# A graph layer in one program: folded mixer weights, centred key weights, split edge weights, and hot columns on ScalarE

## The reference

```python
xn = _layernorm(x, axis=-1)
x = x + gnn(xn, src, dst, edge_weight, ...) + mix(xn[None], ...)[0]
x = x + ffn(_layernorm(x, axis=-1)[None], ...)[0]

# gnn: new_x[src] += edge_weight * xn[dst]; then two 256x256 products around a batch norm and tanh
# mix: qkv = xn @ w_qkv + b_qkv; per head (8 heads of 32):
k = _ln(k, kln_g, kln_b); v = _ln(v, vln_g, vln_b)
kv = einsum('bhnd,bhne->bhde', k, v) / HW
out = einsum('bhnd,bhde->bhne', q, kv)
ret = out + xn
h = gelu(ret @ w1 + b1); mixed = h @ w2 + b2 + xn
# ffn: router over 8 experts, top 2, each expert 256 -> 1024 -> 256 with gelu
```

## Time and profile before

| | |
|---|---|
| median of 3 runs | 2387.26 us |
| the profiled execution | 2384.72 us |
| its span, from first to last instruction | 2383.3 us |
| first put, last put starts | 108.38 us, 1352.15 us |
| experts, full windows from | 1700 us |
| mean granted TensorE clock | 0.891 |

### The profile page before, as it was taken

One profiled execution on the slowest core, in us unless ns is written; L12 is line 12 of the kernel. 1 busy time (PEld: TensorE's weight loads), 2 busy tenths in 40 slices (PEclk: granted clock), 3 DMA queues, 4 the chain that ended last, 5 costly groups with the idle time before them and its releaser, 6 DMA issues. The chain is left out here.

```text
span 2383.3 us, 38273 instructions
## 1 busy us (share of the span) xinstructions
PE 1934.3 (81%) x11227; PEld 1607.3 (67%) x11251; DVE 1713.1 (72%) x5437; ACT 1128.4 (47%) x2236; POOL 1278.8 (54%) x811
## 2 busy tenths in 40 slices
PE   2559997697888878887877266985899999999995
PEld 1437775565665656656666134872799999999995
DVE  4848898687767858673333076888788888988884
ACT  1324443222232332323222114236899999999993
POOL 1447787578778877766777600000355444455542
PEclk8579998799998989888999598665899999999997
DMA  7878877477787787868888673223588888878885
GB/s 232 283 189 153 168 115 126 76 127 121 122 156 132 125 163 134 177 98 192 176 171 165 97 223 112 68 89 107 150 232 233 234 232 233 232 233 234 233 233 167
DMA packets 325710, 401.93 MB, mean 169 GB/s; under 512 B 34841, under 2 KB 267054, under 8 KB 325364
## 3 DMA queue, kind: packets, MB, share of 16 engines
q1 hardware_dynamic: 193822, 256.71, 34.9%
q0 software_dynamic: 103008, 103.83, 32.2%
q10 hardware_dynamic: 28662, 38.84, 5.3%
HBM read 251.12 MB, written 154.55 MB: 170 GB/s over the span
## 5 line engine op out<-in xcount | busy, mean ns | idle before, releaser
L1094 POOL DMA_INDIRECT acc_dram<-third x566 | 914.6, 1616 | 343.0 <-issue 138.6
L2016 POOL DMA_INDIRECT sum_dram<-node,small x112 | 198.2, 1770 | 316.4 <-DVE node L1945 222.7
L1873 PE MATMUL bank<-up_parts 128*128 128x256 f32 x2688 | 334.4, 284 | 2.3 <-DVE up_parts L1903 2.3
L1886 PE MATMUL bank<-down_parts 128*128 128x256 f32 x2688 | 335.4, 284 | 0.0
L1873 PEld LDWEIGHTS bank<-up_parts 128*128 128x128 f32 x2688 | 329.2, 193 | 2.7 <-DVE up_parts L1903 2.7
L1886 PEld LDWEIGHTS bank<-down_parts 128*128 128x128 f32 x2688 | 325.3, 191 | 0.0
L551 PE MATMUL bank<-work,third 128*128 128x256 f32 x1132 | 294.4, 403 | 27.8 <-ACT third L1049 27.7
L1049 ACT ACTIVATE third<-bank 128x512 f32<-128x512 f32 x283 | 168.6, 597 | 290.1 <-DMA acc_dram<-third 234.5
L857 DVE TENSOR_SCALAR third<-fixed,third 128x128 f32<-128x128 f32 x566 | 164.2, 369 | 161.0 <-PE bank L540 142.0
L1998 POOL DMA_INDIRECT node<-xh_dram,small x112 | 135.5, 1209 | 242.2 <-DVE small L1699 208.4
L551 PEld LDWEIGHTS bank<-work,third 128*128 128x128 f32 x1132 | 217.9, 205 | 63.9 <-ACT third L1049 31.6
(11 more groups left out here) (268 smaller groups left out, 3237.4 us busy)
## 6 DMA issues: line engine op xcount, KB each, us to landing
turned<-in_w_up SPq DMA_DIRECT2D x56, 1024.0 KB
turned<-in_w_down SPq DMA_DIRECT2D x56, 1024.0 KB
work<-src_dram SPq DMA_DIRECT2D x141, 256.0 KB
acc_dram<-fixed SPq DMA_DIRECT2D x15, 1280.0 KB, 13.2
work<-xn_dram SPq DMA_DIRECT2D x146, 128.0 KB
work<-acc_dram SPq DMA_DIRECT2D x72, 256.0 KB, 3.5
at_dram<-turned ACTq DMA_DIRECT2D x48, 256.0 KB
work<-at_dram ACTq DMA_DIRECT2D x24, 512.0 KB, 4.5
```

Source lines behind the costliest of these rows:

```text
L1094: e.indirect_dma_start(acc_dram[i], bass.IndirectOffsetOnAxis(put_i[:, t:t + 1], 0), M[:, t % (2 * QUAD), :], None, compute_op=ALU.add).th ...
L1873: k = e.matmul(ps, W1s[:, 2 * b + wp, q, h * P:(h + 1) * P], xTs[:, 2 * b + xp, q, :], start=(q == 0 and (wp, xp) == TERMS[0]), stop=(q == ...
L1886: k = e.matmul(bank[5 + c][:, 0:D], hTs[:, hp, h, c * P:(c + 1) * P], W2s[:, 2 * b + wp, h, :], start=(h == 0 and hp == 0 and wp == 0), st ...
L2016: e.indirect_dma_start(sum_dram, bass.IndirectOffsetOnAxis(slot_i[:, n:n + 1], 0), yb[:, i % 2, c, :], None, compute_op=ALU.add).then_inc( ...
```

## The change

It leaves the node stretch and the experts alone. In the first stretch:

- **Folded mix weights.** After the keys, two more steps multiply KV with the q weights and with Wm1, and add the product to Wm1 and to its bias; q, KV and `ret` are then gone from each chunk. Per chunk remain two up steps and two down steps; the up of chunk c+1 stands ahead of the down of chunk c, and banks and `hT_mix` are doubled.
- **Centred key weights.** The weights and the bias of k and v are centred once per head, so the sums and the centring of each key step go. ScalarE squares straight from the bank, and `kvn` has five slots, with a column of ones at each end.
- **fp32r halves.** The edge weight is split in a rounded part and a rest, in two fp32r matrices `one_lo`, made by one VectorE instruction; TensorE makes two fp32r products for a hot tile in place of one fp32 product.
- **ScalarE ones.** `one_hi` is made on ScalarE as Relu(1 - Abs(n - column)). A is cleared by ScalarE in 13 pieces, three steps long before the first group and piece by piece behind the copies later.
- The first group is 6 nodes wide (294 columns), not 5 (245). The row numbers take one table less, OH has three quads, and the costs by hand are new. M keeps two quads and `at_in` two slots.

The diff, cut to its core:

```diff
-DENSE = ((0, 108, 5), (108, 152, 6), (152, 188, 6), (188, 216, 7))
+DENSE = ((0, 108, 6), (108, 152, 6), (152, 188, 6), (188, 216, 7))
 S_QUADS = 3
+ROW_QUADS = 2
...
+    AI = 2
...
-        mix_steps = sum(3 * KC + (chunk(c)[2] // P) // 2 for c in range(NCH))
-        dense_cost = [2.0, 0.5, 0.5]
+        mix_steps = KC * NCH + sum(len(pair_of(c, m)) > 0 for c in range(NCH) for m in range(KC))
+        dense_cost = [0.6, 0.6, 0.6]
         for a, b, _ in DENSE:
-            dense_cost += [0.8] * (b - a + 2) + [0.7] * (-(-HI // 4) + 1)
+            dense_cost += [0.25] * (b - a + 3) + [0.2] * (-(-HI // 4) + 1)
...
-                in_turn, cost_in_turn, m = in_turn + [0], cost_in_turn + [1.65], m + 1
+                in_turn, cost_in_turn, m = in_turn + [0], cost_in_turn + [0.15], m + 1
...
-        costs = [2.0] + [2.8] * (NT + 4) + [1.0] * 2 + cost_in_turn + [2.4] * (2 * PRODUCTS)
+        costs = [0.6] * 3 + [0.9] * NT + [0.4] * 4 + [0.5] * 4 + cost_in_turn + [0.53] * (2 * PRODUCTS)
...
-                        e.matmul(dense_bank(n)[:, 0:HI * s], one_lo[:, t % 4, :], one_hi[:, t % 3, 0:HI * s],
-                                 start=True, stop=True).then_inc(s_ap, 1)
+                        e.wait_ge(s_away, HOT_DONE[t])
+                        for i_ in range(2):
+                            k = e.matmul(dense_bank(n)[:, 0:even(HI * s)], one_lo[:, t % 4, i_, :], one_hi[:, t % 3, 0:even(HI * s)],
+                                         start=(i_ == 0), stop=(i_ == 1))
+                        k.then_inc(s_ap, 1)
...
-                    e.tensor_reduce(ksum, rows, AX.X, ALU.add).then_inc(s_kvln, 1)
-                    e.wait_ge(s_kvln, KEY_DONE["sum", t])
-                    if t >= 4:
-                        e.wait_ge(s_kvacc, t - 3)
-                    e.scalar_tensor_tensor(out=d3, in0=spread16(ksum), scalar=-1.0 / HD, in1=rows,
-                                           op0=ALU.mult, op1=ALU.add).then_inc(s_kvln, 1)
...
+            for g in range(2):
+                e.wait_ge(s_foldp, g + 1)
+                e.tensor_copy(folded[:, g, :], bank[6 + g][:, 0:D]).then_inc(s_fold, 1)
+                e.tensor_copy(kvar2[:, 0, g:g + 1], bank[6 + g][:, D:D + 1]).then_inc(s_fold, 1)
+            yield
+            e.wait_ge(s_foldp, 3)
+            for m in range(KC):
+                e.tensor_tensor(Wm1[:, m, :], Wm1[:, m, :], bank[6 + m][:, 0:D], ALU.add).then_inc(s_fold, 1)
+            e.tensor_tensor(cols[:, 1, :], cols[:, 1, :], bank[5][:, 0:KC], ALU.add).then_inc(s_fold, 1)
+            yield
...
-            e.memset(A, 0.0).then_inc(s_tables, 1)
+            e.tensor_scalar(far_col, near, -1.0, 1.0, ALU.mult, ALU.add).then_inc(s_tables, 1)
...
-                        e.tensor_scalar(one_lo[:, t % 4, :], iota_p, lo_col[:, t:t + 1], w_c[:, t:t + 1], ALU.is_equal, ALU.mult)
-                        e.tensor_scalar(one_hi[:, t % 3, 0:HI * s], iota_n[:, 0:HI * s], hi_col[:, t:t + 1], None,
-                                        ALU.is_equal).then_inc(s_one, 1)
+                        e.scalar_tensor_tensor(out=one_lo[:, t % 4], in0=iota_p.unsqueeze(1).broadcast_to((P, 2, P)),
+                                               scalar=lo_col[:, t:t + 1], in1=parts_w[:, t, :].unsqueeze(2).broadcast_to((P, 2, P)),
+                                               op0=ALU.is_equal, op1=ALU.mult).then_inc(s_one, 1)
...
-                if g + 1 < NG:
-                    e.wait_ge(s_atp, HC4 * (g + 1))
-                    e.memset(A, 0.0).then_inc(s_clear, 1)
...
+                        e.activation(away[:, t % 2, 0:even(HI * s)], iota_n[:, 0:even(HI * s)], ACT.Abs, bias=far_col[:, t:t + 1]).then_inc(s_away, 1)
...
+                        e.activation(one_hi[:, t % 3, 0:even(HI * s)], away[:, t % 2, 0:even(HI * s)], ACT.Relu, bias=ones[:, 0:1],
+                                     scale=-1.0).then_inc(s_away, 1)
```

More of the change, by code:

```diff
@@ L163, in gps_layer @@
         third = region("third", NT * D, late)
-        work = region("work", 13064, late)
+        work = region("work", 13060 + NG, late)
         src_c = third(EG * P)
         w_c = third(EG * P)
-        trash_minus = third(EG * P)
         dup = third(EG * P)
@@ L360, in dense_bank @@
             return bank[n % 2]
[L363 to L367, removed]
-            mix_uses += [(s_mfin, 4 * c + j + 1) for j in range(chunk(c)[2] // P)]
-        USES = 3 * KC + 4
-        def mix_bank(n):
-            return bank[5 + n % 3]
         quat = [[(0, 1), (1, 1), (2, 1), (3, 1)], [(1, -1), (0, 1), (3, 1), (2, -1)],
@@ new lines, in keys_tensor, with up, down @@
+            for m in range(KC):
+                for g in range(2):
+                    k = e.matmul(bank[6 + m][:, 0:D], folded[:, g, m * P:(m + 1) * P], Wm1[:, g, :], start=(g == 0), stop=(g == 1))
+            k.then_inc(s_foldp, 1)
+            yield
+        def mix_tensor(e):
+            def up(c, m):
+                w = chunk(c)[2]
+                e.wait_ge(s_xr[c % 2], 16 * (c // 2 + 1))
+                if KC * c + m:
+                    e.wait_ge(s_mha, KC * c + m)
+                for q in range(KC):
+                    k = e.matmul(bank[5][:, 0:w], Wm1[:, q, m * P:(m + 1) * P], xnT_ring[:, c % 2, q, 0:w],
+                                 start=(q == 0), stop=(q == KC - 1))
+                k.then_inc(s_mh, 1)
+            def down(t):
+                c, j = t // 4, t % 4
+                e.wait_ge(s_mha, KC * (c + 1))
+                if t >= 2:
+                    e.wait_ge(s_mfin, t - 1)
+                for q in range(KC):
+                    e.matmul(bank[6 + t % 2][:, 0:D], hT_mix[:, c % 2 * KC + q, j * P:(j + 1) * P], Wm2[:, q, :],
+                             start=(q == 0), stop=False)
+                e.matmul(bank[6 + t % 2][:, 0:D], ones_b, b2_b, start=False, stop=True).then_inc(s_mfp, 1)
+            e.wait_ge(s_fold, 7)
+            for m in range(KC):
+                up(0, m)
+                yield
@@ L464, in mix_tensor @@
+                    if len(pair_of(c, m)):
+                        for t in pair_of(c, m):
+                            down(t)
                         yield
@@ L473, in dense_tensor @@
             for g, (a, b, s) in enumerate(DENSE):
-                for i in range(b - a + 2):
-                    t = a + i - 1
+                for i in range(b - a + 3):
+                    t = a + i - 2
                     if a <= t < b:
@@ L587, in keys_vector @@
                 vec.wait()
+                if row is b2row:
+                    for end in (0, 2 * D + 1):
+                        vec.done(e.memset(kvn[:, :, end:end + 1], 1.0))
+                    vec.wait()
                 e.scalar_tensor_tensor(out=row_b, in0=r, scalar=ident[:, 2:3], in1=row_b, op0=ALU.mult, op1=ALU.add).then_inc(s_bias, 1)
@@ L955, in mix_scalar, with clear @@
+                    if len(pair_of(c, m)):
                         yield
         def dense_scalar(e):
-            yield
-            yield
-            yield
-            for g, (a, b, s) in enumerate(DENSE):
-                for i in range(b - a + 2):
+            def clear(k):
+                block = A[:, 4 * k:min(4 * k + 4, HI), :].rearrange("p a b -> p (a b)")
+                return e.activation(block, zeros[:, 0:block.shape[1]], ACT.Copy)
+            e.wait_ge(s_set, SET_ZEROS)
+            e.wait_ge(s_xnTd, 16 * NCH)
```

382 lines of the change are left out of this document (192 added, 190 removed).

## The result

The change makes the kernel slower: 2440.64 us, the median of 4 runs (2438.05 to 2457.46), against 2386.06 us (2382.23 to 2388.74) in the same comparison; ratio 1.0245, interval 1.0197 to 1.0293. The profiled execution took 2439.76 us, its span is 2438.4 us, and its mean clock 0.858. The forecast of 2372 us was wrong, in sign too, and the range ended at 2425.

A forecast was written before the change was run, and what follows sets the result against it. GpSimd's puts, with a floor of 1.86 us each, were taken to bound the first stretch. Terms -11.5, -12, -6 and +17 sum to -12.5 us on 2384.7: 2372 us; 8 in 10 range 2325 to 2425.

The forecast's parts named there:

- The same chain: Hot quads: addition, `select` and `indices`, hot tile, product, base block and next product sum to 7.5 us, under GpSimd's 8.3.
- It has room; 0: ScalarE in hot quads: with Abs and Relu added it does 5.4 us per quad of 8.3; term 0.
- Keys now spread over 43 quads: Key steps: keys fall on 43 quads in place of 32, hidden by puts and landings; term 0, bounds 0 and -24.
- the count: Hot stretch: 216 tiles now fall on 51 quads, where before it was 2.7 on 80 quads.
- The share at half clock: Hot quads: 16% of 51 quads at the lower clock, 8 x 2.1 us: +17 us, bounds 0 and +107.
- rival A: Quads 46 to 96: the dense loop at half clock bounds the stretch, 2419 to 2462 us; chance 0.30.
- Clearing A on ScalarE: Hot stretch: two long puts beside VectorE's clearings go; -11.5 us, bounds 0 and -16.5.
- The rule on shared interfaces: Puts: GpSimd contends with VectorE's two-port or two-input instructions; for `one_lo` at most +91 us, left inside rival A's range.
- The transition: From 391 to 484 us: half of the 24 us lost there comes back, -12 us; bounds -6.7 and -24.
- the fold steps: In key quads: eight small instructions, once; 0.
- Centred keys: Key steps, 174 to 391 us: some 1.4 us of VectorE less per step, hidden; term 0, bounds 0 and -24.
- `ret` and KV gone: From 1020 to 1080 us: q, KV and `ret` go, up runs one chunk ahead; -6 us, bounds 0 and -12.

The follow-up runs named there:

- ring4: The changed kernel with ScalarE's Abs and Relu one tile further ahead, `one_hi` ring four deep, AT left at three slots: 2421.03 us, 1.0104 to the kernel before.
- select_between: The changed kernel with VectorE's program order alone changed, `select` and `indices` behind the tiles dealt ahead of the base block: 2369.57 us, 0.9894 to the kernel before.
- keys_first: The changed kernel with only the costs changed, key steps at half cost, products at 0.42: 2356.24 us, 0.9866 to the kernel before.
- before_hot_late: The kernel before with only its costs changed, key steps 1.7 times as costly, hot tiles dealt as the change deals them: 2477.7 us, 1.0399.
- hot_twice: The changed kernel with the two fp32r products of each hot tile issued twice: 2451.83 us, 1.0248 to the kernel before.
- clear_vector: keys_first with A cleared by VectorE again, four instructions in place of ScalarE's 13 pieces: 2373.1 us, 0.9936 to the kernel before.
- ones_vector: The changed kernel with `one_hi` made on VectorE again, nothing on ScalarE for it: 2436.61 us, 1.0183 to the kernel before.
- ones_ahead: The changed kernel with ScalarE's Abs and Relu two tiles further ahead, `one_hi` ring 5 not 3, AT 2 slots not 3: 2437.31 us, 1.0177 to the kernel before.

## Why the prediction was wrong, by its own steps

*"The same chain is ... 7.5 us. GpSimd needs 8.3 us per quad, so at full clock the loop keeps ahead."* This step failed. The 24 quads with two and two took 9.0 us at full clock and 10.9 at half, the 11 with three and two 10.7 at full clock. The chain as summed held VectorE and TensorE alone. In the quad from 847.24 to 857.60 us its term for the base block, "the next product and its start" and the addition is 2.62 + 0.5 + 0.46 = 3.6 us, and takes 5.5 there, with the wait for ScalarE's ones in it; `select` and `indices` take 2.9 for 2.74, `one_lo` and the second addition 1.3 for 0.88, and the product ahead of the block 0.7 for 0.3. "It has room; 0" for ScalarE went by its busy share: 5.4 us of 8.3. But its 1.08 us per tile stand between the copies into M and the next product, on the path. ring4 puts a price on that order: 20 us on the medians, 34 by the ratios (1.0245 against 1.0104). That `select` and `indices` stand ahead of the second addition was in the chain; what it costs was not seen, and select_between puts it at 71 us, with what the clock gives back.

*"Keys now spread over 43 quads ... Term 0"* failed with it. It was 0 on the belief that the puts set the pace everywhere. Where the hot tiles set it, their stretch takes its 580 us whatever the quads (586, 576, 583 and 591 us in the kernel before, the change, keys_first and before_hot_late), and each quad dealt elsewhere is added: 57 us for eight. The prediction had the two and two in front of it, and the 8.75 us between such blocks in the kernel before, but then went by the 7.5 us of its own sum. One gap was also too few to read: the five quads of this kind before took 9.9 us on the mean. And the count was off: the 216 tiles were said to move from 80 quads to 51, where by the programs 66 quads issue hot products before and 57 after.

*The share at half clock*, 16% of the quads, was read off a mean clock. Of the changed kernel's 53 quads with steps of hot tiles and no transposes 24 ran their block at half, and 0.84 in the windows is below the 0.86 that rival A named. Rival A, at a chance of 0.30, gave 2419 to 2462 us, and 2440 lies amid it; blocks over 10 us apart and puts that wait for the copies into M were its signs, and both came, but the clock was 0.84 and not near 0.6. Its cause holds in part: 17 of 24 quads with two and two were at half, but the 11 with three and two were slow at full clock, hot_twice raised the clock for nothing, and select_between took the wait away and found the clock risen by itself, to 0.89 from 530 to 1000 us. How much of the 71 us that it gave back is the clock and how much the wait is not parted. The Trainium skill, page "TensorE: Matmul & The Clock Gate", section "HAM oscillation — how this bites in real kernels", has such restarts in every pass of a loop with a wait. The trace agrees in part: 24 of these 53 blocks ran so, 1.91 us for 1.05, and the others at full clock.

*Clearing A on ScalarE*, -11.5, was right in mechanism: the changed kernel has no put over 2.1 us. The size is within what the runs can tell: 17 us by clear_vector, with three long puts; the kernel before has the two that were counted, at 722.55 and 869.64 us. The rule on shared interfaces ("GPSIMD Engine Reference", section "1. Specifications", of the Trainium skill) would fit the clearing if this memset runs in a two-port mode, which no run here shows. For the two-input `one_lo` no price shows: a put's mean is 1595 ns with it, and 1616 before, or 1596 without the 11.5 us of the two long puts.

*The transition*, -12, was half moved on. From 391 to 484 us 49 puts go where 33 went, but from 484 to 530 us 17 puts take 46 us, 12 more than at 2.0 each. There stand the fold steps, priced at 0 "in key quads", and the tables; no run parts them. GpSimd waits 5.98 us ahead of the put at 494.95:

```profile
494.95 1.56 POOL L1145 DMA_INDIRECT acc_dram<-third  x1 [5.98 <-DVE third L903]
```

*Centred keys*: 2.01 us per put for 2.09, some 9 us over 108 puts where the prediction had 0, within its bounds. *`ret` and KV gone*, -6: not seen apart from the rest; 1000 to 1177 us was slowed by the hot tiles.

## What to carry to other kernels

When a loop over several engines is dealt out from a table, the path inside one round decides, not any engine's busy share: write the round down once with every engine's program order, and look for what stands between a result and its user. A table of costs is an edit as large as any: here it was worth 87 us one way (before_hot_late) and 84 the other (keys_first), and a change of parts and table together should be timed with the old table too. If a stretch takes the same time however many rounds pass in it, deal as many rounds to it as it will bear.

## What was not expected of the hardware

A stretch that no edit touched, behind the puts, took 9 us more, and 1027 to 1046 us over all kernels here, with TensorE at the lower clock in other places of it (0.50 against 0.86 in the same 24 us of program); so differences of 10 us between single executions say nothing of an edit. And a wait moved from one engine to the other when ScalarE's part was taken away, in ones_vector with no change in length and in ones_ahead with a small one (164.0, 167.3 and 144.5 us), so that ScalarE's part looked innocent by the time alone. VectorE's part, taken away alone, gave its 71 us.
